# Two causal transformer layers on one core: the opening without its start signal, one natural-score wait moved back by one, and another table of gaps

## The reference, cut to what matters

```python
for layer in (0, 1):
    xn = layernorm(x)                                  # over 512, no weights
    q, k, v = xn @ Wq.T, xn @ Wk.T, xn @ Wv.T          # 16 heads of 32
    q, k = rope(q), rope(k)
    p = softmax(causal(q @ k.T * 32 ** -0.5))
    attn = (p @ v) @ Wo.T
    mlp = (silu(xn @ Wgate.T) * (xn @ Wup.T)) @ Wdown.T   # layer 1: each product with its scales
    x = x + attn + mlp
```

## Time and profile before

| | us |
|---|---|
| median of 3 runs | 1902.45 (1900.71 to 1902.92) |
| the profiled execution, its own time | 1899.04 |
| its span in the trace | 1897.3 |
| PE busy | 1801.1 |
| DVE, ACT, POOL busy | 1051.5, 1093.5, 720.5 |

### The profile page before, as it was taken

How to read it: one execution, slowest core, us unless ns; L and a number is a source line. 1 busy time by engine, 2 the same in 40 slices (tenths; PEclk the granted TensorE clock), 3 DMA queues, 4 the chain that set the end, 5 groups by cost and what they waited for, 6 DMA issues and landing times.

```text
span 1897.3 us, 24679 instructions
## 1 busy us (share of the span) xinstructions
PE 1801.1 (95%) x8656; PEld 1335.4 (70%) x8656; DVE 1051.5 (55%) x2368; ACT 1093.5 (58%) x2445; POOL 720.5 (38%) x628
## 2 busy tenths in 40 slices
PE   5899999999999999998999999999999999999989
PEld 4676777677777676766587677777777766777655
DVE  5455557373557373837357374655635655556453
ACT  2575757485237475757536666575732575757573
POOL 2335253343343344424333252525243335343331
PEclk9999999999999999999999999999999999999989
DMA  6213131130131131404152040314111313131201
GB/s 211 78 36 94 46 90 50 33 119 27 56 90 58 44 81 31 114 1 128 52 166 79 23 117 22 85 46 117 46 56 46 83 35 94 46 84 40 67 13 45
DMA packets 66314, 130.32 MB, mean 69 GB/s; under 512 B 7696, under 2 KB 8720, under 8 KB 65168
## 3 DMA queue, kind: packets, MB, share of 16 engines
q1 hardware_dynamic: 66192, 128.75, 23.5%
HBM read 73.67 MB, written 4.19 MB: 41 GB/s over the span
## 4 chain that ended last, share of the span: by engine, by line
PE 77%; DVE 9%; ACT 8%; issue 3%; POOL 2%; DMA 0%; PEldq 0%; SPq 0%; DVEq 0%; ACTq 0%; POOLq 0%
PE D L987 17%; PE G L987 12%; PE U L987 12%; PE OE L987 8%; PE OE L1085 7%; PE SS L1069 6%; PE SS L987 5%; PE OE L1048 3%; PE OE L1069 3%; PE SS L1048 3%; DVE xres L949 2%; ACT OE L672 2%; ACT pr L691 2%; ACT SS L672 2%; DVE OE L907 2%
## 5 line engine op out<-in xcount | busy, mean ns | idle before, releaser
L949 DVE TENSOR_TENSOR xres<-D,xres 128x512 f32<-128x512 f32 x352 | 239.6, 689 | 220.6 <-PE D L987 218.1
L691 ACT ACTIVATE pr<-SS 128x512 f32<-128x512 f32 (+3 forms) x512 | 238.5, 500 | 89.2 <-PE SS L1069 59.4
L785 POOL TENSOR_TENSOR hl<-tt,hh 128x512 fp32r<-128x512 f32 x108 | 139.2, 1289 | 345.1 <-ACT hh L709 344.8
L672 ACT ACTIVATE OE<-OE,mp 128x384 f32<-128x384 f32 (+3 forms) x256 | 204.1, 798 | 79.4 <-DVE mp L907 77.5
L907 DVE CUSTOM_DVE_ANT_0 OE<-OE,mask 128x384 f32<-128x384 f32 (+3 forms) x256 | 220.7, 871 | 50.7 <-PE OE L1048 49.4
L803 POOL TENSOR_SCALAR_AFFINE_SELECT pr<-pr 128x512 f32<-128x512 f32 x128 | 81.2, 635 | 285.2 <-ACT pr L691 285.2
L987 PE MATMUL G<-xh,wgh 128*128 128x512 f32 x432 | 174.6, 404 | 15.6 <-DVE tt L960 12.4
L1069 PE MATMUL SS<-QS,KS 98*128 98x512 f32 (+2 forms) x512 | 177.2, 387 | 11.5 <-ACT pr L691 5.2
L907 DVE CUSTOM_DVE_ANT_0 SS<-SS,mask 128x128 f32<-128x128 f32 (+3 forms) x256 | 169.3, 674 | 30.1 <-PE SS L1048 29.4
L672 ACT ACTIVATE SS<-SS,mp 128x128 f32<-128x128 f32 (+3 forms) x256 | 162.2, 635 | 40.4 <-DVE mp L907 38.6
L987 PE MATMUL D<-wdh,hh 128*128 128x512 f32 x432 | 171.1, 396 | 1.4 <-issue 1.0
(11 more groups left out here) (121 smaller groups left out, 3812.4 us busy)
## 6 DMA issues: line engine op xcount, KB each, us to landing
KS<-pr SPq DMA_DIRECT2D x128, 192.0 KB, 3.3
QS<-pr SPq DMA_DIRECT2D x128, 192.0 KB, 3.2
raw<-in_wgate_dram SPq DMA_DIRECT2D x28, 512.0 KB, 3.7
raw<-in_wup_dram SPq DMA_DIRECT2D x28, 512.0 KB, 3.7
raw<-in_wdown_dram SPq DMA_DIRECT2D x27, 512.0 KB, 3.7
raw<-in_wqk_dram SPq DMA_DIRECT2D x16, 512.0 KB, 3.4
trig<-in_rope_dram SPq DMA_DIRECT2D x4, 1024.0 KB, 5.0
xres<-in_x_dram SPq DMA_DIRECT2D x4, 1024.0 KB, 6.6
```

What stands on the lines that cost most here:

```text
L672: act.activation(s, s, ACT.Exp, bias=mp[:, c, at:at + 1], scale=-1.0, accum_out=se[:, c, at:at + 1]) \
L691: act.activation(weights(i)[:, h, skip:W], SB[(i * HG + h) % 3][:, skip:W], ACT.Exp, scale=-1.0) \
L785: pool.tensor_tensor(hl[:, fc, :], tt[:, (blk * nfc + fc) % 2, :], hh[:, fc, :].bitcast(F32), ALU.subtract) \
L949: dve.tensor_tensor(xres[:, rt, :], d[:, :], xres[:, rt, :], ALU.add).then_inc(sem["v_dfree"], 1)
```

## The change

Four edits and the tables:

- `s_ready` is removed, and the four waits for it. The credits are added as before. SP issues the loads of the scales and of the first down, gate and up weights right behind the others; DVE's two fills at its start wait for nothing.
- ACT's queue begins with a copy of 16 columns of the identity into `ex`, behind `s_const`; the table load of ACT goes in front of it.
- `nat` 17, the first double score that uses OE, waits for the exponential of `nat` 15, no longer for that of `nat` 16.
- Other digits in `PACE` for all 16 turns (217 of the 878 pieces stand before another item), other values in `LATER`. The pieces keep their order among each other.

```diff
@@ PACE @@
-        ("01003100110010102032053212121111101010010001000200100000000010000000000000000000000000000000000003",
+        ("01002200110100102032053212120211101010010001000110100000000010000000000000000000000000000000000102",
...
-LATER = (("02r0000l0040ap002o010100", "0102900dx02024E100"),
-         ("02a0224mj0200ba02p000100", "0100b00ba000078"))
+LATER = (("00n0003c0000ap0025000000", "010ca008C01025E000"),
+         ("04c06000c0300b001i000000", "511bc00cf000178"))
@@ sync @@
             sp.dma_start(trig[:, :, :], rope[0]).then_inc(sem["d_rope"], 16)
-            sp.wait_ge(s_ready, 1)
             sp.dma_start(sc[:, :, :], scales).then_inc(d_const, 16)
@@ scalar @@
-            act.wait_ge(s_ready, 1)
+            act.wait_ge(s_const, 3)
+            act.copy(ex[:, :], ident[:, 0:HG * TPC])
             act.wait_ge(sem["raw2"], 16)
@@ gpsimd @@
-            pool.wait_ge(s_ready, 1)
             split_first(0)
@@ vector @@
-            dve.wait_ge(s_ready, 1)
             dve.memset(mm[:, :, :], 0.0)
             dve.memset(KS[STACK:P, :, :].bitcast(F32), 1.0)
@@ tensor @@
-            pe.sem_inc(s_ready, 1)
             pe.wait_ge(s_const, 4)
...
-                    pe.wait_ge(sem["a_nat"], n("a_nat", -1 if t > HG * TPC + 1 else 0))
+                    pe.wait_ge(sem["a_nat"], n("a_nat", -1))
```

More of the change, by code:

```diff
@@ L288 @@
     (
[L289 to L292, removed]
-        ("01003100110010102032053212121111101010010001000200100000000010000000000000000000000000000000000003",
-         "00002010010010010103022212111112031011020101000011000001101001000000000000000010000000000000000002",
-         "02100020100010110023111202121112120030100100101010100000101000000000001000000000000000000000000002",
-         "0010000101000200011211020111101101001100000100000010000000000000000000000000000000000000010015040"),
-    ),
@@ L298 @@
-    (
[L299 to L306, removed]
-    ),
-)
@@ L309 @@
-LATER = (("02r0000l0040ap002o010100", "0102900dx02024E100"),
-         ("02a0224mj0200ba02p000100", "0100b00ba000078"))
+        ("40000120010010100021111201120312031010101010011002100000110010001000001100000010010000000000000201",
+         "00000210010010020103020321302121112001001002001101100010100110000000001000000010010011000010000021",
+         "00102002010110002012121203020212213011101001000111000001003001000100010100000000000000000000000000",
+         "00400111012010101102022111121212021101010010001010200000100010000000010100000210010101001703ag040"),
@@ new lines @@
+        ("01002200110100102032053212120211101010010001000110100000000010000000000000000000000000000000000102",
+         "00010200010100010112031212111112120111011010100011100000101001000000000000000010000000000000000020",
+         "20100020100011010112031203111112120040010001001001100000010010000000000100000000000000000000000001",
+         "0200000101000200020111120111101101001010000000200000000000000000000000000000000000000000010015040"),
+    ),
+    (
+        ("40001111000101030011111112211202111110010110200100300000101010000000000000000010100000000000000200",
+         "00102102002010020101111211212121112010001101002001100010110101000000001000000011001001001000000011",
+         "40000020010101001012120311221121212021001001000110000000101010000000010010000010110001001000000001",
+         "003010101011002010120321011212120220101000100112010000001110100000000100100010100100100007037j220"),
+        ("04100111000101100212140311210121202010010101001020000000000010000000000000000000000000000000000030",
+         "00000201001000101013121212111112120030020001001200100000010000000000001100000000000000000000000102",
+         "00100201110011010112030303021112121020110001000001000000010010000000000100000000000000000000000003",
+         "1000200011100011101114120301010100000000000000000000000000000000000000000000000000000000d000"),
+    ),
+)
@@ L473, in two_layers @@
         d_const = ctx.enter_context(nc.semaphore("d_const"))
-        s_ready = ctx.enter_context(nc.semaphore("s_ready"))
         s_vconst = ctx.enter_context(nc.semaphore("s_vconst"))
```

## The result

| | before, us | after, us |
|---|---|---|
| median, 4 runs each | 1901.71 (1900.71 to 1902.92) | 1878.76 (1876.81 to 1878.96) |
| the profiled execution, its own time | 1899.04 | 1878.86 |
| its span | 1897.3 | 1877.1 |

The changed kernel is faster: ratio 0.9877, 95% interval 0.986 to 0.9894. The direction was forecast and the size was not: 1891.5 us was predicted and 1886 was the lower end of the range. The profiled executions differ by 20.2 us, where the sum had 11.0.

The account below looks back on a forecast made before the run. PE was taken to bound the kernel, with only its late starts to win. Opening 6.7, wait of score 17 1.5 and table 2.8 sum to 11.0 us: 1902.45 - 11.0 = 1891.5 us, range 1886 to 1898.

Parts of the forecast that it names:

- What bounds the kernel: PE, busy 1801.1 of 1897.3 us; its work stays, so only its late starts, 223 us in all, can be won.
- The opening: Program start: without the start signal DVE's fills and statistics run earlier, and 6.7 us carry to the end; bounds 2.5 to 7.5.
- Rival 2: Opening pays less: DVE's start or one of nine unpaused loads becomes the bound; 1895.6 us, chance 0.07.
- The wait of score 17: PE's score 17 in 16 turns: visible lateness 2.8 us, of which 1.5 taken as gain; bounds 0 to 2.8.
- The table: Moved pieces in all turns: 2.8 us gained, a third of the 9 us upper bound; loss of 4 at most.
- The 15 gaps: Gaps of 0.3 us or more before items gaining a piece, 9 us together; closing all was the table's upper bound.
- the weight steps: Weight splits moved by LATER: no gain counted, only a danger that small DVE operations meet GpSimd ones anew.
- Rival 3: Opening and table pay more: gaps before a fall of the clock go, and the fall too; 1886.0 us, chance 0.10.
- Rival 1: The table gives nothing: closed gaps reappear at the next score or where a piece was given up; 1896.3 us, chance 0.17.
- Rival 4: Slower: moved weight splits spread the DVE and POOL collision to more log steps, 2.3 us each on PE; chance 0.03.
- The collision that was expected to stay: Log step of (1,1) turn 0: DVE's 16-column operation beside POOL's multiplication stays above 1 us; nothing counted.
- The last turn: From score 17 on as before, some 24 us late with the clock at 0.50, no pieces left to put there.

Follow-up runs that it names:

- the kernel with the late fill: The changed kernel with DVE's two fills moved from its start to the step that splits the first weights: 1878.66 us, ratio to before 0.9885.
- the nine: Pieces taken from in front of score 17 in nine turns; put back there, against the kernel before with new tables and new wait, old opening: 1890.33 us.
- the run for the halves: Kernel before with new wait, new digits and moved weight steps only up to each turn's last natural score: 1913.78 us, ratio 1.0075.

## Why the prediction was right about the sign and wrong about the size

**What bounds the kernel: right.** PE's work stayed, and the difference of the spans is the difference of PE's lateness with the opening.

**The opening: right.** 6.7 us predicted, 6.4 measured, 6.1 to 6.2 at the first projection. The fill stood at 0.90, the statistics at 5.44 as predicted; the first transpose at 11.94 and the first projection at 18.50 came half a microsecond later than 11.4 and 17.9. The prediction checked whether POOL's split would be *ready* in time and not whether it would now *coincide* with the normalisation, the question that it did ask of the log steps. Rival 2 fell: none of the nine loads became late for its user. They are not untouched, though: the first weights, which landed at 7.75 before, landed at 7.95 in after and at 8.88 in the kernel with the late fill. POOL's split starts at 9.07 and 10.00 by that, and the two normalisations beside it take 1.47 and 2.03 us.

**The wait of score 17: the old lateness was the wrong price.** Taken by itself it was read slightly low (1.5 for 2.9, the bound being 2.8). The step that failed is that it entered the sum as a term of its own, priced by how late score 17 was under the *old* table. The old table hid this wait with a piece in front of 17; the prediction even says so ("whose new wait allows that: 9 of 16 turns take a piece away there"), and still counted only what was left visible. What the wait would have cost under the new table, 10.6 us of lateness and 13.0 of time, was nowhere in the sum.

**The table: mis-sized, and looked for in the wrong place.** The term was 2.8, a third of 9 us, with 9 as the upper bound; beyond the wait alone, tables and wait together are worth 11.8. So the sum should have been 6.4 + 2.9 + 11.8 = 21.1 and not 6.7 + 1.5 + 2.8 = 11.0: nearly all that was missing is missing here. Three parts of this step failed.

First, the discount to a third. The 15 gaps closed from 9.0 to 2.5 us. That "most gaps are of 0.5 us against a piece of 0.9" was given as a reason against; but the number of pieces is the same, so the length of one adds no work where it fills a gap. Sorted by size, the gaps of 0.6 to 1 us, those of about a piece, went from 42 to 27 between before and the kernel with tables and wait (31.8 to 20.3 us), and the gaps from 0.3 to 0.6 us stayed (114 and 112 of them, 47 us in both). In sum, then, the table closed gaps about as long as a piece; that is a count from two traces, and no run tested it.

Second, the item as the unit. A gap was ascribed to the item in front of which it was seen, and only an item that *gains* a piece was allowed to lose its gap. In fact that class did not improve (20.0 to 22.0), and the two others gave 14.7 us. An example, from the timeline of the kernel before:

```profile
86.08 0.50 PE L987 MATMUL G<-xh,wgh 128*128 128x512 f32 x1 [0.73 <-DVE tt L960]
...
87.12 0.51 PE L1048 MATMUL OE<-KS,QS 96*128 96x512 f32 x2
```

This is the gap of 1.10 us counted at score 17 of (0,0) turn 0, which loses one of two pieces. PE waits not with the score but with the gate piece in front of it, for DVE's reading of the bank. The piece went elsewhere, and so did the wait: 0.03 us are left. Pieces are not only filler; they wait for DVE as the scores wait for ACT, and moving them away from a place where they wait is a gain. Part of it shows in the row G <- DVE tt of the waits, 12.4 us before and 8.5 after. The 8.5 is a low reading: the three other kernels with new tables and wait have 10.1 to 10.3, so some 2 us are the tables'. In one place such a wait only moved: 1.85 us in front of the last item of (0,1) turn 2 stand in after two items later with 1.84:

```profile
849.60 0.51 PE L983 MATMUL G<-xh,wgh 128*128 128x512 f32 x1 [1.84 <-DVE tt L957]
```

Third, the weight steps. They were counted at nothing and bring 3.6 of the 11.8 us. By what wait they bring it is not shown.

**The rivals.** Rival 3 named the right direction and the wrong cause: a fall of the clock that goes. It does not go. Behind the opening 42 us of before and 47 us of after run at the lower level, 1.2 GHz, in 10 and 11 stretches. Rival 1, that closed gaps reappear at the next score, is what the tables did without their wait, at score 17. Rival 4 did not come. The collision that was expected to stay did stay; the log step of (1,1) turn 0 in after, against the earlier trace rows:

```profile
1500.91 1.34 DVE L921 TENSOR_TENSOR ex<-se,ex 128x16 f32<-128x16 f32 x1
1500.92 2.53 POOL L776 TENSOR_TENSOR raw<-raw,ds 128x512 f32<-128x512 f32 x2
...
1502.28 1.20 DVE L923 SCALAR_TENSOR_TENSOR lse<-ex,y 128x16 f32<-128x16 f32 x1
...
1505.39 0.45 PE L1051 MATMUL D<-ident,mm 128*128 128x128 f32 x1 [2.44 <-DVE xres L946]
```

Over all log steps the slowed small operations are 9 after and 13 before, 6.1 and 8.8 us above their usual length: some of them are no longer met by POOL, the opposite of rival 4. That is not what the moved weight steps bring: with the new digits and the weight steps at their old items it is 10 operations and 6.6 us, against 9 and 6.1 with both tables, so at most half a microsecond of the 3.6.

**The last turn: nearly right.** It was forecast as before from score 17 on. Its lateness is 24.4 us, 26.0 before, and its clock still falls, for 10.2 us of these twelve where all twelve were low before, against the earlier trace rows (length, busy us of PE, PEld, DVE, ACT, POOL, granted clock, DMA):

```profile
1818.00:1824.00 6.00, 5.78 (x15) 3.75 (x14) 1.50 (x8) 5.74 (x19) 1.90 (x3) 0.55 0.00 0
1824.00:1830.00 6.00, 4.44 (x31) 1.78 (x35) 0.00 (x0) 1.15 (x3) 0.63 (x1) 0.60 0.02 5
```

**The base and the range.** The prediction of 1891.5 was 12.7 us too high against 1878.76. 10.0 of it are the sum (21.0 at equal clock against 11.0). The other 2.7 are the base: the sum was taken from the median of three runs, 1902.45, which lies 3.0 us above the 1899.4 at which the fit puts the kernel at a clock of 0.989, and after's median 0.4 above its own. The lower end of all bounds, 1883.2, was still too high, because the bounds of the two coupled terms were drawn from the visible gaps of the old trace. Three slips moved nothing: the upper end of 1904.0 takes the opening at 2.5 us and not at the 4 written beside it; half of nine us less 0.5 us at one in ten of 185 items is a loss of 4.8 and not 4; and six of the 16 steps of score 17, not seven, are late by under 0.03 us.

**What stays open.** Which of the moved pieces bring the 6.5 us that the new table is worth without the nine, in which half of a turn, and by which wait the weight steps bring their 3.6, was not settled; the run for the halves failed by the late weights.

## What to carry to other kernels

When a change removes a wait and at the same time takes away the work that covered it, price the wait without its cover: remove the filler on paper and ask how late the waiting instruction would then be, rather than how late it is in the old trace. Two edits of this kind are one term, and their bound is that of the hidden wait. When filler is moved, look at three things: the gap it goes to, the gap it leaves, and the waits that it has itself, since a filler that waits is a gap that goes wherever it goes.

## What the runs showed of the hardware that was not expected

- The time of an unchanged program moves with the mean granted clock of the execution: 57 executions of before, 1895.2 us at 0.992 to 1905.5 at 0.986, 1.5 us for each 0.001. One profiled execution, or a median of three, can stand 3 us off for that reason alone, a good part of what the smaller edits here are worth. With the executions put on one line by their clock, 0.75 us of scatter was left.
- DVE's normalisation of 128 x 512 (one SBUF tile as input and one as output) took 1.00 us for two tiles alone and 1.47, 2.03 and 2.06 us in the kernels in which POOL's split of the first weights ran beside it; with POOL held back it was 1.00 again, and the next tile 0.86 instead of 0.54. The Trainium skill (SBUF — State Buffer, Who interferes with whom) says that a `tensor_scalar` can enter a mode that takes the port pair that DVE shares with GpSimd, and that one of the two then blocks for a whole instruction. These rows agree that the two interfere; the two tiles together lost at most 1.06 us, less than one of the two POOL instructions took (2.48 to 2.67 us for both).
- A small operation loses as much as a large one: DVE's product of 16 columns took 0.17 us in the median and 1.17 (before) and 1.34 us (after) beside POOL's multiplication, seven to eight times its length.
